# Tridiagonalisation: the next column as K times a packed vector less R, with work reordered around it

## The chip, the cores and the metric

The kernel runs on one core of one Trainium2 chip. The metric is device microseconds of one execution, as the median of several runs. A core has a matrix engine (TensorE, PE in the rows), a vector engine (VectorE, DVE), an activation engine (ScalarE, ACT), GpSimd (POOL) and a queue for transfers (SyncE, SP). They run their own instruction streams and meet at semaphores.

## The reference

Two graph layers on x of 128 batches x 128 nodes x 128 features, each behind a layer norm and a clipping at zero, and each added to x. What matters here is the first:

```
deg    = sum(A, 0) + sum(A, 1) - diag(A)
L_norm = d_inv_sqrt * (diag(deg) - A) * d_inv_sqrt
_, U   = eigh(L_norm)                     # 128 x 128, symmetric
out    = U @ (relu((U.T @ h) @ W1 + b1) @ W2 + b2)
```

The second layer is two graph convolutions and four small LSTMs over windows of 1 to 4 nodes. All is fp32.

## The kernel before

The eigenvectors are computed on the chip: the matrix is brought to tridiagonal form by 127 Householder steps (`STEPS`), the eigenvalues are found by counting sign changes and the eigenvectors by twisted factorisations, two refinements follow, and then come the two layers, batch group by batch group, with TensorE busy almost throughout. Only the tridiagonalisation is changed.

`householder(k)` exists twice, in TensorE's stream (from line 591) and in VectorE's (from line 897); ScalarE's part stands in a loop at lines 420 to 431. A step k works on the "live" columns k+1 to 127, so its row operations get shorter by one column per step. The order is written out by hand, with a semaphore for every dependence, also between two instructions of VectorE (`step()` counts them in `hv`, and `dve.wait_ge(hv, n)` waits for the n-th).

One step goes round like this:

- x, the current column below the diagonal, lies in column 128 of `ident`. VectorE writes it at L951.
- TensorE multiplies it out (L596: x's leading element and its sum of squares on all partitions; L598: the whole of x as a row).
- ScalarE takes the root of the sum (L424, `two_sigma`) and half the leading element's size (L425, `half_x`), copies the row to `uB` (L428) and stores the off-diagonal element (L431).
- VectorE forms u (L915) in `UC[:, k, 2]`; beside it lie x masked below the diagonal (`UC[:, k, 1]`, written by `prepare_sign`, L968) and minus the mask (`UC[:, k, 0]`).
- TensorE forms the row product u'A (L601, into bank 1) and A u (L603, into bank 2).
- VectorE in the meantime forms the denominator (L919, L922), the leading element of u on all partitions (`u_t`, L925), the reciprocal h (L927), and h times the three columns of UC (L930, into HB, HUM, HU).
- L935 multiplies u'A by the row of u and sums it, to K (K3). It is followed by a read of the accumulator, which has a row of its own in the trace.
- L939 to L951 work out the next column x before the matrix itself is updated: V1, Z, T2, NHP, then x. L954, L956 and L960 update the matrix A (twice) with wB between. L967, L968 (`prepare_sign`) and L974 (`prepare_row`, SGE) prepare the sign for the next u.

From step 16 on (`BN_LAG`) each step also takes the layer norm statistics of one batch, `x_statistics` (L895), which have nothing to do with the step and are put in the queue to use it. L912 forms ACOL, the next column of A below the diagonal, for T2.

Behind step 16 (`LEAF`) the leading 16 x 16 block is handed to GpSimd, which runs 16 sweeps on it beside everything else (ending with the copy at L410). VectorE reads its result, a sign, at L1343 in the second refinement.

Of the kernel before, what the change touches and what calls it, by code (L numbers as in the profile page):

```python
# [10 lines left out]
N = 128  # L11
# [19 lines left out]
SKIPS = 4  # L31
# [28 lines left out]
def build(nc, t_in, out):  # L60
    with ExitStack() as ctx:
# [3 lines left out]
        def sem(name):  # L65
            return ctx.enter_context(nc.semaphore(name))
# [58 lines left out]
        x_in = [sem(f"x_in{c}") for c in range(X_CHUNKS)]  # L125
        tables = sem("tables")
        weights_in = sem("weights_in")
        small_in = sem("small_in")
        w_turned = sem("w_turned")
        w_kept = sem("w_kept")  # L130
        small_turned = sem("small_turned")
# [39 lines left out]
        u_ready = sem("u_ready")  # L171
        p_ready = sem("p_ready")
        a_ready = sem("a_ready")
        leaf_ready = sem("leaf_ready")
        leaf_sign = sem("leaf_sign")
        to_pe = sem("to_pe")
# [11 lines left out]
        block = ctx.enter_context(nc.Block())  # L188

        STEPS = N - 1  # L190
        ST, DEN, SGE1, SGE, K3, NHP, V1, T2, Z, ACOL = range(10, 20)
        HB, HUM, HU = range(20, 23)

        def two_sigma(k):
            return sc[:, 24 + k % 2:25 + k % 2]
# [4 lines left out]
        def half_x(k):  # L200
            return sc[:, 28 + k % 2:29 + k % 2]

        def live(k):
            return slice(k + 1, N)

# [58 lines left out]
        @block.sync  # L266
        def _(sp):
            sp.dma_start(adj[:], t_in["adj"]).then_inc(adj_in, 16)
            for c in range(X_CHUNKS):
                r = slice(c * BATCH // X_CHUNKS, (c + 1) * BATCH // X_CHUNKS)  # L270
                sp.dma_start(X[:, r, :], x_dram[:, r, :]).then_inc(x_in[c], 16)
            for c, name in enumerate(("L1_gnn_Wih", "L1_gnn_Whh")):
                for p in range(SKIPS):
                    sp.dma_start(w_nat[:, c, p], t_in[name][p].rearrange("(g u) h -> u g h", g=4)).then_inc(weights_in, 16)
            for t, name in ((W1, "L0_gnn_W1"), (W2, "L0_gnn_W2"), (Wg0, "L1_gnn_Wg0"), (Wg1, "L1_gnn_Wg1")):
                sp.dma_start(t[:], t_in[name]).then_inc(small_in, 16)
            for t, name in ((b2B, "L0_gnn_b2"), (bg0B, "L1_gnn_bg0"), (bg1B, "L1_gnn_bg1")):
                sp.dma_start(t[:], t_in[name].rearrange("(a d) -> a d", a=1).to_broadcast([N, D])).then_inc(small_in, 16)
            sp.dma_start(b1[:], t_in["L0_gnn_b1"].rearrange("(d a) -> d a", a=1)).then_inc(small_in, 16)
            for c, name in enumerate(("L1_gnn_bih", "L1_gnn_bhh")):  # L280
                sp.dma_start(bias_nat[:, c, :], t_in[name].rearrange("p (g u) -> (p g) u", g=4)).then_inc(small_in, 16)
            for g in range(GROUPS):
                if g >= RING:
                    sp.wait_ge(x1_ready[g % STREAMS], (g - RING) // STREAMS + 1)
                sp.dma_start(batches(ring[g % RING]), x_dram[:, g * GB:(g + 1) * GB, :]).then_inc(ring_in[g % RING], 16)
            with nc.sync.Fori(0, ROUNDS) as it:
                for i in range(STREAMS):
                    b = bass.ds(it * (STREAMS * GB) + i * GB, GB)
                    sp.wait_ge(sum_ready[i], it + 1)
                    sp.dma_start(out_dram[:, b, :], X[:, b, :]).then_inc(stored, 16)  # L290
            sp.wait_ge(stored, 16 * ROUNDS * STREAMS)
# [124 lines left out]
        def _(act):  # L416
            act.wait_ge(rs_in, 1)
            nc.scalar.activation(m[5][:], m[4][:], ACT.Sqrt).then_inc(rs_out, 1)
            for k in range(STEPS):
                t = k + 1  # L420
                if k >= 2:
                    act.wait_ge(e_ready, k - 1)
                act.wait_ge(s_ready, k + 1)
                nc.scalar.activation(two_sigma(k), banks[7][:, 1:2], ACT.Sqrt, scale=4.0).then_inc(sigma_ready, 1)  # L424
                nc.scalar.activation(half_x(k), banks[7][:, 0:1], ACT.Abs, scale=0.5).then_inc(sigma_ready, 1)  # L425
                if t + 1 < N:
                    act.wait_ge(xb_ready, k + 1)
                    nc.scalar.activation(uB[:, k % 2, t + 1:N], banks[0][:, t + 1:N], ACT.Copy).then_inc(row_ready, 1)  # L428
                act.wait_ge(sg_ready, k + 1)
                act.wait_ge(sigma_ready, 2 * k + 1)  # L430
                nc.scalar.activation(eB[:, k:k + 1], sign(k), ACT.Identity, scale=two_sigma(k)).then_inc(e_ready, 1)  # L431
# [146 lines left out]
        def _(pe):  # L578
# [54 lines left out]
            nc.tensor.matmul(B[4], QU, QV, start=True, stop=False)  # L633
            nc.tensor.matmul(B[4], ident[:, 0:N], ident[:, 0:N], start=False, stop=True).then_inc(q_pe, 1)

            pe.wait_ge(weights_in, 16 * 2 * SKIPS)
            for c in range(2 * SKIPS):
                if c >= 2:
                    pe.wait_ge(w_kept, c - 1)
# [1 line left out]
                    last = nc.tensor.transpose(banks[c % 2][:, q * D:(q + 1) * D], w_nat[:, c // SKIPS, c % SKIPS, q, :],  # L641
                                               ident[:, 0:N])
                last.then_inc(w_turned, 1)
            pe.wait_ge(small_in, 16 * 10)
            pe.wait_ge(w_kept, 2 * SKIPS)
            nc.tensor.transpose(banks[0][:, 0:N], adj[:], ident[:, 0:N])
            K = 4 * SKIPS
# [176 lines left out]
        def _(dve):  # L824
# [4 lines left out]
            def op(ins):  # L829
                t.did(ins)  # L830
                t.last(dve)
# [8 lines left out]
            def S(i, n=1):  # L840
                return sc[:, i:i + n]
# [38 lines left out]
            V.tensor_copy(sc[:, 40:41], sc[:, 1:2]).then_inc(x_ready, 1)  # L880

            op(V.tensor_scalar(UC[:, 0:N - 1, 0], below[:, 1:N], -1.0, None, ALU.mult))
            h = Tally(hv)

            def step(ins):

                h.did(ins)
                return h.n

            def x_statistics(b):

                if b % (BATCH // X_CHUNKS) == 0:
                    dve.wait_ge(x_in[b // (BATCH // X_CHUNKS)], 16)
                V.bn_stats(stats[:, b, :], X[:, b, :]).then_inc(bn_done, 1)  # L895

            def householder(k, before):
# [8 lines left out]
                sigma2, sg = two_sigma(k), sign(k)  # L906
                x_t, s = banks[7][:, 0:1], banks[7][:, 1:2]

                if k >= BN_LAG:
                    x_statistics(k - BN_LAG)  # L910
                dve.wait_ge(a_ready, k + 1)
                step(V.tensor_tensor(S(ACOL), A[:, nxt], below[:, nxt], ALU.mult))  # L912
                dve.wait_ge(sigma_ready, 2 * k + 1)
                dve.wait_ge(hv, before)
                V.scalar_tensor_tensor(out=u_c, in0=S(SGE), scalar=sigma2, in1=x_c,  # L915
# [3 lines left out]
                n_st = step(V.tensor_scalar(S(ST), s, TINY, None, ALU.add))  # L919
                V.tensor_scalar(sg, x_t, 0.0, 0.5, ALU.is_ge, ALU.subtract).then_inc(sg_ready, 1)  # L920
                dve.wait_ge(hv, n_st)
                n_neg = step(V.scalar_tensor_tensor(out=S(DEN), in0=half_x(k), scalar=sigma2, in1=S(ST),  # L922
                                                    op0=ALU.mult, op1=ALU.add))
                dve.wait_ge(sg_ready, k + 1)
                n_ut = step(V.scalar_tensor_tensor(out=u_t, in0=sg, scalar=sigma2, in1=x_t, op0=ALU.mult, op1=ALU.add))  # L925
                dve.wait_ge(hv, n_neg)
                n_h = step(V.reciprocal(h_k, S(DEN)))  # L927
                dve.wait_ge(hv, n_h)
                dve.wait_ge(u_ready, k + 1)
                n_nh = step(V.tensor_tensor(S(HB, 3), UC[:, k, :], h_k.to_broadcast([N, 3]), ALU.mult))  # L930

                dve.wait_ge(pb_ready, k + 1)
                if t + 1 < N:
                    dve.wait_ge(row_ready, k + 1)
                n_k = step(V.tensor_tensor_reduce(out=wB[:, live(k)], in0=banks[1][:, live(k)], in1=uk[:, live(k)],  # L935
                                                  scale=h_k, scalar=0.0, op0=ALU.mult, op1=ALU.add,
                                                  accum_out=S(K3)))
                dve.wait_ge(hv, n_nh)
                n_v = step(V.tensor_tensor(S(V1), S(HB), u_t, ALU.mult))  # L939
                dve.wait_ge(hv, n_k)  # L940
                n_z = step(V.scalar_tensor_tensor(out=S(Z), in0=u_t, scalar=S(K3), in1=B[1][:, nxt],
                                                  op0=ALU.mult, op1=ALU.subtract))
                dve.wait_ge(p_ready, k + 1)
                dve.wait_ge(hv, n_v)
                n_t2 = step(V.scalar_tensor_tensor(out=S(T2), in0=banks[2][:, 0:1], scalar=S(V1), in1=S(ACOL),  # L945
                                                   op0=ALU.mult, op1=ALU.add))
                n_nhp = step(V.scalar_tensor_tensor(out=S(NHP), in0=banks[2][:, 0:1], scalar=-1.0, in1=h_k,
                                            op0=ALU.mult, op1=ALU.mult))
                dve.wait_ge(hv, n_t2)

                V.scalar_tensor_tensor(out=x_c, in0=S(HUM), scalar=S(Z), in1=S(T2),  # L951
                                       op0=ALU.mult, op1=ALU.add).then_inc(x_ready, 1)
                dve.wait_ge(hv, n_nhp)
                step(V.scalar_tensor_tensor(out=A[:, live(k)], in0=uk[:, live(k)], scalar=S(NHP), in1=A[:, live(k)],  # L954
                                                  op0=ALU.mult, op1=ALU.add))
                n_wb = step(V.scalar_tensor_tensor(out=wB[:, live(k)], in0=uk[:, live(k)], scalar=S(K3),  # L956
                                                   in1=banks[1][:, live(k)], op0=ALU.mult, op1=ALU.subtract))
                n_sge1 = prepare_sign(k + 1) if k + 1 < STEPS else None
                dve.wait_ge(hv, n_wb)
                V.scalar_tensor_tensor(out=A[:, live(k)], in0=wB[:, live(k)], scalar=S(HU), in1=A[:, live(k)],  # L960
                                       op0=ALU.mult, op1=ALU.add).then_inc(a_ready, 1)
                return prepare_row(k + 1, n_sge1) if k + 1 < STEPS else None
# [546 lines left out]
```

## Time and profile before

| what | value |
|---|---|
| median of 3 runs | 1530.33 us (1529.59 to 1530.63) |
| the profiled execution: its own time, its span | 1528.6 us, 1526.9 us |
| PE, DVE, ACT, POOL busy, share of the span | 78%, 74%, 52%, 33% |
| stretch 200 to 392 us (tridiagonalisation): PE, DVE, ACT busy | 138.74, 185.87, 46.90 us of 192 |
| stretch 674 to 1526 us (the layers): PE, DVE busy | 838.10, 479.69 us of 852 |
| TensorE's granted clock in the tridiagonalisation | 1.00 of full speed |

Times in rows are microseconds from the start of the span. An instruction's listed length is from its start to its end; instructions of one engine overlap, so that the next one can start before the listed end of the one in front. Busy time counts an engine as busy while an instruction is under way in it, also when that instruction is one element long and mostly latency.

### The profile page before, as it was taken

What the parts mean: (1) busy time and instruction counts of PE and PEld (TensorE: products, weight loads), DVE (VectorE), ACT (ScalarE), POOL (GpSimd) and SP (SyncE); (2) the same over time, 40 slices, a digit from 0 to 9 for tenths busy, and PEclk for the clock granted to TensorE, in tenths of its full rate; (3) what the DMA queues carried; (4) which work ended last, traced back from release to release, by engine and by line L of the source; (5) the groups of instructions that cost most, each with busy time, mean ns of one, the idle gap of its engine ahead of it and who ended that gap; (6) DMA issues with size and microseconds to landing.
All of it is one profiled execution on the core that took longest, in us unless ns stands there. A gap on an engine that the chain in (4) does not pass through costs nothing.

```text
span 1526.9 us, 26214 instructions
## 1 busy us (share of the span) xinstructions
PE 1196.6 (78%) x7121; PEld 1070.4 (70%) x7121; DVE 1127.4 (74%) x6077; ACT 796.6 (52%) x2572; POOL 511.0 (33%) x1426
## 2 busy tenths in 40 slices
PE   5666777777616600069999999999999999999998
PEld 4555666666515500058889899898998989989897
DVE  8999999999999999977757655555465555645545
ACT  1222222222319900002478687786877868778676
POOL 0288888888888888830000200000000000000000
PEclk9999999999959955569999999999999999999999
DMA  9300000000000000003100000000000000000001
GB/s 268 77 1 0 1 1 1 1 1 1 1 0 2 1 0 1 0 14 97 56 1 1 28 0 14 14 0 28 0 14 14 0 27 0 14 13 0 28 1 29
DMA packets 43625, 28.76 MB, mean 19 GB/s; under 512 B 1520, under 2 KB 39440, under 8 KB 43536
## 3 DMA queue, kind: packets, MB, share of 16 engines
q1 hardware_dynamic: 43536, 27.81, 6.7%
q8 instruction: 27, 0.44, 0.1%
q14 instruction: 62, 0.51, 0.1%
HBM read 19.42 MB, written 8.39 MB: 18 GB/s over the span
## 4 chain that ended last, share of the span: by engine, by line
PE 57%; DVE 38%; issue 3%; ACT 2%; ACTq 0%; DVEq 0%
PE bank L794 13%; PE bank L784 10%; PE bank L789 8%; PE bank L797 7%; PE bank L601 6%; DVE PV L1192 5%; DVE RC L1186 4%; DVE PV L1122 2%; DVE wB L935 2%; PE bank L714 2%; PE bank L766 2%; PE bank L758 2%; PE bank L722 2%; DVE sc L945 2%; PE bank L729 2%
## 5 line engine op out<-in xcount | busy, mean ns | idle before, releaser
L794 PE MATMUL bank<-spare,wT 128*128 128x256 f32 (+2 forms) x1408 | 311.2, 321 | 0.0
L530 ACT ACTIVATE PV<-bank,bias 128x256 f32<-128x256 f32 (+2 forms) x704 | 304.9, 436 | 0.0
L530 ACT ACTIVATE BIG<-bank,bias 128x128 f32<-128x128 f32 (+2 forms) x544 | 228.2, 419 | 120.2 <-PE bank L797 101.2
L794 PEld LDWEIGHTS bank<-spare,wT 128*128 128x128 f32 x1408 | 234.8, 191 | 13.2
L784 PE MATMUL bank<-spare,wT 128*128 128x128 f32 (+2 forms) x1088 | 228.1, 320 | 4.1 <-DVE spare L1429 2.7
L1415 DVE TENSOR_TENSOR BIG<-BIG,PV 128x128 f32<-128x128 f32 (+2 forms) x192 | 63.0, 328 | 206.0 <-ACT BIG L530 205.9
L784 PEld LDWEIGHTS bank<-spare,wT 128*128 128x128 f32 x1088 | 168.7, 190 | 22.5 <-DVE spare L1429 9.1
L797 PE MATMUL bank<-spare,wT 128*128 128x128 f32 (+2 forms) x768 | 169.7, 303 | 0.0
L424 ACT ACTIVATE sc<-bank 128x1 f32<-128x1 f32 x127 | 21.7, 171 | 262.3 <-PE bank L596 262.3
L596 PE MATMUL bank<-ident 128*128 128x2 f32 x254 | 74.4, 363 | 92.8 <-DVE ident L951 91.6
L789 PE MATMUL bank<-spare,wT 128*128 128x128 f32 (+2 forms) x768 | 141.6, 307 | 3.7 <-DVE spare L1427 1.2
L381 POOL TENSOR_TENSOR leaf<-leaf 128x1 f32<-128x1 f32 x240 | 136.0, 567 | 20.0
L538 ACT ACTIVATE spare<-spare 128x256 f32<-128x256 f32 (+2 forms) x352 | 134.6, 382 | 6.9 <-DVE spare L1418 6.9
L596 PEld LDWEIGHTS bank<-ident 128*128 128x128 f32 x254 | 63.7, 311 | 103.8 <-DVE ident L951 102.3
L1412 DVE TENSOR_TENSOR spare<-BIG,PV 128x256 f32<-128x256 f32 (+2 forms) x160 | 60.8, 380 | 96.2 <-ACT PV L530 96.1
L797 PEld LDWEIGHTS bank<-spare,wT 128*128 128x128 f32 x768 | 125.2, 191 | 3.3
L789 PEld LDWEIGHTS bank<-spare,wT 128*128 128x128 f32 x768 | 113.8, 191 | 14.1 <-DVE spare L1427 10.8
L379 POOL TENSOR_SCALAR leaf<-leaf 128x1 f32<-128x1 f32 x240 | 102.1, 426 | 23.3
L601 PE MATMUL bank<-A,UC 128*128 128x127 f32 (+63 forms) x254 | 87.5, 442 | 15.2 <-DVE UC L915 3.6
L588 PE MATMUL bank<-ones,sc 128*128 128x1 f32 x2 | 0.6, 349 | 120.2 <-DVE sc L1252 120.2
L601 PEld LDWEIGHTS bank<-A,UC 128*128 128x128 f32 x254 | 63.6, 311 | 38.8 <-DVE UC L915 38.8
L1192 DVE SCALAR_TENSOR_TENSOR PV<-RC,m,PV 128x4 f32<-128x4 f32 x508 | 90.7, 220 | 0.0
(393 smaller groups left out, 2756.7 us busy)
## 6 DMA issues: line engine op xcount, KB each, us to landing
spare<-in_x SPq DMA_DIRECT2D x32, 256.0 KB, 4.1
out<-X SPq DMA_DIRECT2D x32, 256.0 KB, 2.4
spare<-in_L_gnn_Wih SPq DMA_DIRECT2D x4, 256.0 KB, 5.1
spare<-in_L_gnn_Whh SPq DMA_DIRECT2D x4, 256.0 KB, 5.0
W<-in_L_gnn_W SPq DMA_DIRECT2D x2, 64.0 KB, 2.5
Wg<-in_L_gnn_Wg SPq DMA_DIRECT2D x2, 64.0 KB, 2.2
adj<-in_adj SPq DMA_DIRECT2D x1, 64.0 KB, 1.8
X<-in_x SPq DMA_DIRECT2D x4, 0.5 KB, 17.1
```

The lines of the kernel that those rows point to most:

```text
L379: op(TS(am[:, i + 1:i + 2], rho[:, i:i + 1], ne16[:, i:i + 1], am[:, i + 1:i + 2], ALU.mult, ALU.add))
L381: op(TT(rho[:, i + 1:i + 2], am[:, i + 1:i + 2], neg16[:, 0:1], ALU.pow))
L530: last = nc.scalar.activation(gate_out[q][i][:, 0:T], gate(i, q, T), ACT.Tanh if q == GATE_G else ACT.Sigmoid, bias=bias[:, at:at + 1])
L538: nc.scalar.activation(tS[i][:, 0:T], cS[i][:, 0:T], ACT.Tanh).then_inc(tanh_ready[i], 1)
L596: nc.tensor.matmul(banks[7][:, 0:2], x_wide, ident[:, t:N + 1:N - t], start=True, stop=True).then_inc(s_ready, 1)
L601: nc.tensor.matmul(banks[1][:, live(k)], u_c.to_broadcast([N, N]), A[:, live(k)], start=True, stop=True).then_inc(pb_ready, 1)
L784: last = nc.tensor.matmul(gate(i, q, T), wT[:, 0, p - 1, q * D:(q + 1) * D], xt, start=True, stop=(j == 0))
L789: last = nc.tensor.matmul(gate(i, q, T), wT[:, 1, p - 1, q * D:(q + 1) * D], hS[i][:, 0:T], start=False, stop=True)
L794: last = nc.tensor.matmul(gate(i, q, T), wT[:, 0, p - 1, q * D:(q + 1) * D], xt, start=True, stop=(j == 0))
L797: last = nc.tensor.matmul(gate(i, q, T), wT[:, 1, p - 1, q * D:(q + 1) * D], hS[i][:, 0:T], start=False, stop=True)
L1192: s.did(V.scalar_tensor_tensor(out=nx, in0=RC[:, last + lane:last + lane + live], scalar=M[2][:, row:row + 1], in1=nx, op0=ALU.mult, op1=A ...
L1415: V.tensor_tensor(gI[i][:, 0:T], gI[i][:, 0:T], gG[i][:, 0:T], ALU.mult).then_inc(cell_part[i], 1)
```

## The change

- L912 (ACOL) leaves VectorE. ScalarE computes it as a copy of A's column with the mask column as its scale, between L425 and the copy of the row; it waits for `a_ready`. A semaphore `acol_ready` tells VectorE.
- `UC[:, k, 0]` holds the mask instead of minus the mask.
- The product of h with three columns becomes two instructions: HUM, HU = h times two columns, and HV, HG = u_t times h times (mask, masked x), a tensor_scalar with two scalars that are read from columns.
- The next column was HUM * (u_t K - b) + (p V1 + ACOL), b being the element of bank 1, in four instructions behind K (V1, Z, T2, x). It becomes HG * K - R, with PT = b * HUM - ACOL, R = p * HV + PT: three instructions behind K.
- NHP is computed behind x instead of in front of it; wB comes before A's first update instead of behind it.
- `x_statistics` moves from the start of the step to behind the reciprocal; the wait for ScalarE's copy of the row (`row_ready`) moves from L935 to the product in front of it.
- ScalarE's wait for its own stores (`e_ready`) goes, and the loads of the small weights count on the semaphore of the large ones; TensorE waits for all of them at once, behind the eigenvectors' preparation.

```diff
 # ScalarE
-                if k >= 2:
-                    act.wait_ge(e_ready, k - 1)
                 act.wait_ge(s_ready, k + 1)
                 nc.scalar.activation(two_sigma(k), banks[7][:, 1:2], ACT.Sqrt, scale=4.0).then_inc(sigma_ready, 1)
                 nc.scalar.activation(half_x(k), banks[7][:, 0:1], ACT.Abs, scale=0.5).then_inc(sigma_ready, 1)
+                act.wait_ge(a_ready, k + 1)
+                nc.scalar.activation(S_(ACOL), A[:, t:t + 1], ACT.Copy, scale=below[:, t:t + 1]).then_inc(acol_ready, 1)
 # TensorE
-            pe.wait_ge(weights_in, 16 * 2 * SKIPS)
+            pe.wait_ge(weights_in, 16 * (2 * SKIPS + 10))
...
-            pe.wait_ge(small_in, 16 * 10)
 # VectorE
-            op(V.tensor_scalar(UC[:, 0:N - 1, 0], below[:, 1:N], -1.0, None, ALU.mult))
+            op(V.tensor_copy(UC[:, 0:N - 1, 0], below[:, 1:N]))
...
-                if k >= BN_LAG:
-                    x_statistics(k - BN_LAG)
-                dve.wait_ge(a_ready, k + 1)
-                step(V.tensor_tensor(S(ACOL), A[:, nxt], below[:, nxt], ALU.mult))
                 dve.wait_ge(sigma_ready, 2 * k + 1)
...
                 n_h = step(V.reciprocal(h_k, S(DEN)))
+                if k >= BN_LAG:
+                    x_statistics(k - BN_LAG)
                 dve.wait_ge(hv, n_h)
                 dve.wait_ge(u_ready, k + 1)
-                n_nh = step(V.tensor_tensor(S(HB, 3), UC[:, k, :], h_k.to_broadcast([N, 3]), ALU.mult))
-
-                dve.wait_ge(pb_ready, k + 1)
                 if t + 1 < N:
                     dve.wait_ge(row_ready, k + 1)
-                n_k = step(V.tensor_tensor_reduce(out=wB[:, live(k)], in0=banks[1][:, live(k)], in1=uk[:, live(k)],
-                                                  scale=h_k, scalar=0.0, op0=ALU.mult, op1=ALU.add,
-                                                  accum_out=S(K3)))
-                dve.wait_ge(hv, n_nh)
-                n_v = step(V.tensor_tensor(S(V1), S(HB), u_t, ALU.mult))
-                dve.wait_ge(hv, n_k)
-                n_z = step(V.scalar_tensor_tensor(out=S(Z), in0=u_t, scalar=S(K3), in1=B[1][:, nxt],
-                                                  op0=ALU.mult, op1=ALU.subtract))
+                n_hu = step(V.tensor_tensor(S(HUM, 2), UC[:, k, 1:3], h_k.to_broadcast([N, 2]), ALU.mult))
+                n_hv = step(V.tensor_scalar(S(HV, 2), UC[:, k, 0:2], u_t, h_k, ALU.mult, ALU.mult))
+
+                dve.wait_ge(pb_ready, k + 1)
+                dve.wait_ge(acol_ready, k + 1)
+                step(V.tensor_tensor_reduce(out=wB[:, live(k)], in0=banks[1][:, live(k)], in1=uk[:, live(k)],
+                                            scale=h_k, scalar=0.0, op0=ALU.mult, op1=ALU.add, accum_out=S(K3)))
+                dve.wait_ge(hv, n_hu)
+                n_pt = step(V.scalar_tensor_tensor(out=S(PT), in0=B[1][:, nxt], scalar=S(HUM), in1=S(ACOL),
+                                                   op0=ALU.mult, op1=ALU.subtract))
+                dve.wait_ge(hv, n_pt)
                 dve.wait_ge(p_ready, k + 1)
-                dve.wait_ge(hv, n_v)
-                n_t2 = step(V.scalar_tensor_tensor(out=S(T2), in0=banks[2][:, 0:1], scalar=S(V1), in1=S(ACOL),
-                                                   op0=ALU.mult, op1=ALU.add))
+                n_r = step(V.scalar_tensor_tensor(out=S(R), in0=banks[2][:, 0:1], scalar=S(HV), in1=S(PT),
+                                                  op0=ALU.mult, op1=ALU.add))
+                dve.wait_ge(hv, n_r)
+                V.scalar_tensor_tensor(out=x_c, in0=S(HG), scalar=S(K3), in1=S(R),
+                                       op0=ALU.mult, op1=ALU.subtract).then_inc(x_ready, 1)
                 n_nhp = step(V.scalar_tensor_tensor(out=S(NHP), in0=banks[2][:, 0:1], scalar=-1.0, in1=h_k,
-                                            op0=ALU.mult, op1=ALU.mult))
-                dve.wait_ge(hv, n_t2)
-
-                V.scalar_tensor_tensor(out=x_c, in0=S(HUM), scalar=S(Z), in1=S(T2),
-                                       op0=ALU.mult, op1=ALU.add).then_inc(x_ready, 1)
-                dve.wait_ge(hv, n_nhp)
-                step(V.scalar_tensor_tensor(out=A[:, live(k)], in0=uk[:, live(k)], scalar=S(NHP), in1=A[:, live(k)],
-                                                  op0=ALU.mult, op1=ALU.add))
+                                                    op0=ALU.mult, op1=ALU.mult))
                 n_wb = step(V.scalar_tensor_tensor(out=wB[:, live(k)], in0=uk[:, live(k)], scalar=S(K3),
                                                    in1=banks[1][:, live(k)], op0=ALU.mult, op1=ALU.subtract))
+                dve.wait_ge(hv, n_nhp)
+                n_a = step(V.scalar_tensor_tensor(out=A[:, live(k)], in0=uk[:, live(k)], scalar=S(NHP), in1=A[:, live(k)],
+                                                  op0=ALU.mult, op1=ALU.add))
```

## Rows read from the trace of the kernel before

**Rows 1.** The chain of work that ended last, stretch 13 to 392 us, shares by line

```profile
by line: PE bank L601 22.7%; DVE wB L935 8.7%; DVE sc L945 7.3%; issue 6.8%; DVE ident L951 6.4%; DVE A L960 6.0%; DVE UC L915 6.0%; DVE A L954 6.0%; DVE wB L956 5.8%; DVE sc L912 3.7%; PE bank L596 2.7%; DVE sc L939 2.3%; DVE sc L947 2.2%;
```

**Rows 2.** Line L951: count, ns shortest/median/longest, first and last start

```profile
L951 DVE SCALAR_TENSOR_TENSOR ident<-sc x127: 211/219/278, 14.6 to 391.2; 128x1 f32<-128x1 f32 x127
```

**Rows 3.** Order of time, one step near 65 columns: start, length, engine, line, operation

```profile
206.41 0.22 DVE L951 SCALAR_TENSOR_TENSOR ident<-sc 128x1 f32<-128x1 f32 x1
206.55 0.28 DVE L954 SCALAR_TENSOR_TENSOR A<-uB,sc,A 128x66 f32<-128x66 f32 x1
...
207.07 0.28 DVE L960 SCALAR_TENSOR_TENSOR A<-wB,sc,A 128x66 f32<-128x66 f32 x1
...
207.27 0.15 DVE L974 TENSOR_TENSOR sc<-sc,ident 128x1 f32<-128x1 f32 x1
207.34 0.28 DVE L895 BATCH_NORM_STATS2 stats<-X 128x6 f32<-128x128 f32 x1
207.36 0.17 ACT L424 ACTIVATE sc<-bank 128x1 f32<-128x1 f32 x1 [2.00 <-PE bank L596]
...
207.54 0.14 DVE L912 TENSOR_TENSOR sc<-A,below 128x1 f32<-128x1 f32 x1
207.60 0.21 DVE L915 SCALAR_TENSOR_TENSOR UC<-sc,ident 128x1 f32<-128x1 f32 x1
...
207.86 0.69 PE L601 MATMUL bank<-A,UC 128*128 128x65 f32 x2
...
208.17 0.16 DVE L927 RECIPROCAL hB<-sc 128x1 f32<-128x1 f32 x1
...
208.37 0.16 DVE L930 TENSOR_TENSOR sc<-UC,hB 128x3 f32<-128x3 f32 x1
208.59 0.28 DVE L935 CUSTOM_DVE_ANT_0 wB<-bank,uB,hB 128x65 f32<-128x65 f32 x1
208.80 0.08 DVE L935 DVE_READ_ACCUMULATOR2_ANT sc<- 128x1 f32 x1
...
209.06 0.22 DVE L945 SCALAR_TENSOR_TENSOR sc<-bank,sc 128x1 f32<-128x1 f32 x1
209.19 0.15 DVE L947 SCALAR_TENSOR_TENSOR sc<-bank,hB 128x1 f32<-128x1 f32 x1
209.31 0.22 DVE L951 SCALAR_TENSOR_TENSOR ident<-sc 128x1 f32<-128x1 f32 x1
```

**Rows 4.** Order of time, VectorE, a step near 106 columns

```profile
80.21 0.22 DVE L951 SCALAR_TENSOR_TENSOR ident<-sc 128x1 f32<-128x1 f32 x1
...
81.53 0.21 DVE L915 SCALAR_TENSOR_TENSOR UC<-sc,ident 128x1 f32<-128x1 f32 x1
...
82.59 0.33 DVE L935 CUSTOM_DVE_ANT_0 wB<-bank,uB,hB 128x106 f32<-128x106 f32 x1
```

**Rows 5.** Order of time, VectorE, a step at 14 columns

```profile
351.83 0.22 DVE L951 SCALAR_TENSOR_TENSOR ident<-sc 128x1 f32<-128x1 f32 x1
...
353.00 0.22 DVE L915 SCALAR_TENSOR_TENSOR UC<-sc,ident 128x1 f32<-128x1 f32 x1
...
353.91 0.23 DVE L935 CUSTOM_DVE_ANT_0 wB<-bank,uB,hB 128x14 f32<-128x14 f32 x1
```

**Rows 6.** Order of time, VectorE, step 15, which has no statistics

```profile
59.07 0.22 DVE L951 SCALAR_TENSOR_TENSOR ident<-sc 128x1 f32<-128x1 f32 x1
...
60.33 0.22 DVE L915 SCALAR_TENSOR_TENSOR UC<-sc,ident 128x1 f32<-128x1 f32 x1
...
61.41 0.33 DVE L935 CUSTOM_DVE_ANT_0 wB<-bank,uB,hB 128x112 f32<-128x112 f32 x1
```

**Rows 7.** Order of time, VectorE, a tensor_scalar with two scalars from columns

```profile
662.34 0.29 DVE L1335 TENSOR_SCALAR sc<-sc 128x2 f32<-128x2 f32 x1
```

**Rows 8.** Order of time, the end of GpSimd's leaf work and VectorE's first reading

```profile
662.45 0.21 POOL L410 COPY leaf<-leaf 128x1 f32<-128x1 f32 x1 [0.23 <-POOL leaf L408]
...
670.56 0.21 DVE L1343 SCALAR_TENSOR_TENSOR sc<-sc,leaf 128x1 f32<-128x1 f32 x1
```

More of the change, by code:

```diff
@@ L127, in build @@
         weights_in = sem("weights_in")
-        small_in = sem("small_in")
         w_turned = sem("w_turned")
@@ L173, in build @@
         a_ready = sem("a_ready")
+        acol_ready = sem("acol_ready")
         leaf_ready = sem("leaf_ready")
@@ L190, in build @@
         STEPS = N - 1
-        ST, DEN, SGE1, SGE, K3, NHP, V1, T2, Z, ACOL = range(10, 20)
-        HB, HUM, HU = range(20, 23)
+        ST, DEN, SGE1, SGE, K3, NHP, PT, R, ACOL = range(10, 19)
+        HUM, HU, HV, HG = range(20, 24)
         def two_sigma(k):
@@ L204, in live, with S_ @@
             return slice(k + 1, N)
+        def S_(i):
+            return sc[:, i:i + 1]
         d16, e16 = leaf[:, 0:16], leaf[:, 16:32]
@@ L275, in _ @@
             for t, name in ((W1, "L0_gnn_W1"), (W2, "L0_gnn_W2"), (Wg0, "L1_gnn_Wg0"), (Wg1, "L1_gnn_Wg1")):
-                sp.dma_start(t[:], t_in[name]).then_inc(small_in, 16)
+                sp.dma_start(t[:], t_in[name]).then_inc(weights_in, 16)
             for t, name in ((b2B, "L0_gnn_b2"), (bg0B, "L1_gnn_bg0"), (bg1B, "L1_gnn_bg1")):
-                sp.dma_start(t[:], t_in[name].rearrange("(a d) -> a d", a=1).to_broadcast([N, D])).then_inc(small_in, 16)
-            sp.dma_start(b1[:], t_in["L0_gnn_b1"].rearrange("(d a) -> d a", a=1)).then_inc(small_in, 16)
+                sp.dma_start(t[:], t_in[name].rearrange("(a d) -> a d", a=1).to_broadcast([N, D])).then_inc(weights_in, 16)
+            sp.dma_start(b1[:], t_in["L0_gnn_b1"].rearrange("(d a) -> d a", a=1)).then_inc(weights_in, 16)
             for c, name in enumerate(("L1_gnn_bih", "L1_gnn_bhh")):
-                sp.dma_start(bias_nat[:, c, :], t_in[name].rearrange("p (g u) -> (p g) u", g=4)).then_inc(small_in, 16)
+                sp.dma_start(bias_nat[:, c, :], t_in[name].rearrange("p (g u) -> (p g) u", g=4)).then_inc(weights_in, 16)
             for g in range(GROUPS):
@@ L921, in householder @@
                 dve.wait_ge(hv, n_st)
-                n_neg = step(V.scalar_tensor_tensor(out=S(DEN), in0=half_x(k), scalar=sigma2, in1=S(ST),
+                n_den = step(V.scalar_tensor_tensor(out=S(DEN), in0=half_x(k), scalar=sigma2, in1=S(ST),
                                                     op0=ALU.mult, op1=ALU.add))
@@ L925, in householder @@
                 n_ut = step(V.scalar_tensor_tensor(out=u_t, in0=sg, scalar=sigma2, in1=x_t, op0=ALU.mult, op1=ALU.add))
-                dve.wait_ge(hv, n_neg)
+                dve.wait_ge(hv, n_den)
                 n_h = step(V.reciprocal(h_k, S(DEN)))
+                if k >= BN_LAG:
+                    x_statistics(k - BN_LAG)
                 dve.wait_ge(hv, n_h)
                 dve.wait_ge(u_ready, k + 1)
-                n_nh = step(V.tensor_tensor(S(HB, 3), UC[:, k, :], h_k.to_broadcast([N, 3]), ALU.mult))
@@ L956, in householder @@
                 n_wb = step(V.scalar_tensor_tensor(out=wB[:, live(k)], in0=uk[:, live(k)], scalar=S(K3),
                                                    in1=banks[1][:, live(k)], op0=ALU.mult, op1=ALU.subtract))
+                dve.wait_ge(hv, n_nhp)
+                n_a = step(V.scalar_tensor_tensor(out=A[:, live(k)], in0=uk[:, live(k)], scalar=S(NHP), in1=A[:, live(k)],
+                                                  op0=ALU.mult, op1=ALU.add))
                 n_sge1 = prepare_sign(k + 1) if k + 1 < STEPS else None
-                dve.wait_ge(hv, n_wb)
+                dve.wait_ge(hv, max(n_a, n_wb))
```

## Prediction, made before the change was run

> **What bounds the kernel now.** I read the chain that ended last first, limited to the tridiagonalisation: it alternates between TensorE's product for p (L601) and a long tail of small VectorE instructions [rows 1]. There is one such loop for each of 127 steps, and L951, which writes the new column x, runs from 14.6 to 391.2 us, so a step is (391.2 - 14.6) / 126 = 2.99 us [rows 2]. What follows this stage is VectorE work again, so each microsecond of the stage goes to the end. Next I read single steps in order of time, and cut one at three instructions: x (L951), u (L915), the row product with its sum K (L935).
>
> The step with some 65 live columns [rows 3] has these stretches. **x to u** takes 1.19 us (206.41 to 207.60). Two ways run side by side: the matmul and ACT's root L424, which starts 0.95 after x, lasts 0.17 and hands over in 0.04 (the gap between L601's end at 208.55 and L935 at 208.59), so 1.16; and VectorE's own queue, which gets to u at 1.19. With 106 columns the stretch takes 1.32, with 14 it takes 1.17 [rows 4, 5]: above some 65 columns VectorE's queue sets it, below that the floor of 1.16. **u to K** takes 0.99 and ends 0.04 behind L601, so TensorE sets it; 1.06 with many columns, 0.91 with few [rows 3 to 5], because L601 gets shorter. VectorE has slack there: it starts L930 at 208.37 and could go on. **K to x** takes 0.72.
>
> Three habits of VectorE are to be seen in [rows 3]. An independent instruction starts 0.08 us before the listed end of the one in front: L912 is 0.14 long and L915 starts 0.06 later; statistics are 0.28 long and L912 starts 0.20 later. One that reads the result of the one in front starts 0.04 behind its end (L927, 0.16 long, to L930: 0.20). An instruction with one scalar read from a column is 0.21 to 0.22 long at one element (L915, L945), and one with a constant 0.15 (L947).
>
> **Part 1, x to u.** Behind x the queue is now NHP, wB, A's first update, the sign work, A's second update, SGE, u. NHP starts 0.14 after x, as L954 does now; wB 0.07 later (0.15 - 0.08). wB and the first update only change places, so from the first of them to L960 it stays 0.52 (206.55 to 207.07). L960 to L974 is 0.20, and u, which reads L974's result, comes 0.15 + 0.04 = 0.19 later. Sum 0.14 + 0.07 + 0.52 + 0.20 + 0.19 = 1.12. That is under the floor, so the floor of 1.16 holds: gain 0.03 at 65 columns. The stretch grew by 0.13 from there to 106 columns (1.32 - 1.19), so the new sum there is 1.12 + 0.13 = 1.25: gain 0.07. At 14 columns the floor already holds: gain 0. The first 16 steps have no statistics: 1.26 now [rows 6], by the same sum with 112 columns 1.27: I call it nothing. The statistics (0.20) and L912 (0.06) leave this stretch, but NHP (0.07) comes in and the wait for SGE (0.12 more than its spacing of 0.07), which statistics had covered, is laid bare.
>
> **Part 2, u to K.** L915 to the reciprocal L927 is 0.57 and unchanged. Behind it now: the statistics (0.16 - 0.08 = 0.08 after L927), the product for HUM and HU (0.20 later), HV and HG (0.08 later, by L930's 0.16), and K's instruction. HV and HG come from one instruction with two scalars read from columns, u_t and h. The step has none, but the trace does, later: L1335 on two elements is 0.29 long [rows 7], so its follower comes 0.21 later. Sum 0.57 + 0.08 + 0.20 + 0.08 + 0.21 = 1.14, and VectorE, not TensorE, sets the stretch. The gap behind the reciprocal that statistics are to fill is only 0.20 wide, and they take 0.28 of queue there; the slack in front of K was 0.22 at most (208.37 to 208.59), and HV eats it. Loss: 1.14 - 1.06 = 0.08 at 106 columns, 0.15 at 65, 0.23 at 14. Without statistics (first 16 steps) it is 0.57 + 0.20 + 0.08 + 0.21 = 1.06 against 1.08 now [rows 6]: hidden behind L601.
>
> HV's price is the term that decides. From below it is 0.07, the spacing of an instruction with constants; from above the 0.21. I take 0.21, since L1335 is the same form on the same number of elements, and one scalar from a column visibly costs 0.06 to 0.07 here, spacing included. 
>
> **Part 3, K to x.** Three dependent instructions: PT starts with the read of the accumulator, 0.21 after K's instruction; R 0.21 + 0.04 = 0.25 later; x another 0.25 later. Sum 0.71 against 0.72. The present order has five instructions there, but the last pair, T2 to x, is already 0.25 apart (209.06 to 209.31) with NHP inside the gap, so taking NHP and V1 away shortens nothing. R reads p no earlier than T2 did. I take 0.01 per step, 1.3 us.
>
> **Part 4, the rest.** ACT's new multiplication for ACOL needs A's second update, which ends at 207.35, just as L424 starts, and is first read behind K at 208.80: over a microsecond of cover. Queued behind it on ACT is the copy of x's row, which HUM's instruction now waits for; if that came late, each 0.1 us would cost 11 us over 111 steps, but both operands are there early. The wait for e_ready on ACT names old stores and ended nothing. The single weight semaphore delays TensorE only behind this stage, when those loads are long over.
>
> **Sum.** Net per step: 0.08 - 0.07 = +0.01 at 106 columns (step 21), 0.15 - 0.03 = +0.12 at 65 (step 62), +0.23 at 14 (step 113), about +0.25 at the last. With straight lines between: 5 x 0.01 + 41 x 0.065 + 51 x 0.175 + 13 x 0.24 = 14.8 us, less 1.3: **+13.5 us**. The profiled execution took 1528.6 us, so 1542.1; the median of the runs is 1.7 above that execution: **1544 us**. A loss here is exposed whole. A gain after step 16 would not be: GpSimd's leaf work, started behind step 16, ends at 662.66, and VectorE reads its sign at 670.56 [rows 8], so 7.9 us of gain at most.
>
> **Rivals.**
> - *HV as cheap as with constants* (0.07). Then u to K is 1.00: losses 0, 0.01 and 0.09, net -0.07, -0.02, +0.09. Sum -0.3 - 1.8 + 1.8 + 1.3 - 1.3 = about 0: 1530 us, no change. This is what the page's 75 ns would make of it. Against it: L1335's length. Chance 0.14.
> - *Faster: the statistics vanish in the gap behind the reciprocal, and HV is cheap.* u to K by VectorE is 0.57 + 0.20 + 0.07 + 0.07 = 0.91, never above TensorE's, and only part 1's gain is left: -3.2 - 1.3 = -4.5, under the cap of 7.9: 1526 us. It decides once that stretch takes under about 1.00. For it: the gap is as wide as the statistics' spacing. Against it: the reciprocal's own 0.08 comes first. Chance 0.12.
> - *Slower still: HUM's instruction starts only when the statistics are complete* (0.28 + 0.04 instead of 0.20), or part of that, because it has three waits. Up to 0.12 x 111 = 13 us more, 1557; half of it 1551. Against it: nothing it reads comes from them. Chance 0.12.
> - The forecast: 0.62.
>
> Slower by over 0.2% (3 us, about what a measurement can tell from no change) gets 0.62 + 0.12 = 0.74, within 0.2% 0.14, faster 0.12. The likeliest case alone spans 1536 to 1548. The range of 8 in 10 reaches down to the no-change case and up past half of the last rival: 1528 to 1553.
>
> **What the changed profile would show.** x to u: 1.25 and then flat at 1.16 to 1.17 from about 75 columns down; that would hold part 1. u to K: flat at about 1.14 whatever the columns, with L601 long done; if it still shrinks with the columns, HV is cheap and the forecast wrong. HV's instruction 0.29 long with K's 0.21 behind it. K to x unchanged. ACOL's activation done before u. The stage from 14.6 to about 405 instead of 391 us.

## The result and the profile after

The changed kernel takes 1537.88 us (median of 5 runs, 1537.44 to 1538.21) against 1530.15: ratio 1.005, interval 1.0039 to 1.0062, so 7.7 us slower. The profiled execution took 1537.93 us with a span of 1536.2. One of the ten executions of after_stats_front below took 2912.92 us; why is open, and it is left out of that kernel's ratio.

First the line that writes x, as in [rows 2], then the chain by line in the same stage, as in [rows 1], both of the kernel after:

```profile
L947 DVE SCALAR_TENSOR_TENSOR ident<-sc x127: 219/220/269, 14.6 to 399.0; 128x1 f32<-128x1 f32 x127
```

```profile
by line: PE bank L599 9.8%; DVE sc L944 7.5%; DVE ident L947 7.5%; DVE UC L913 7.2%; DVE sc L933 6.8%; issue 6.7%; DVE sc L920 6.2%; DVE wB L937 5.3%; DVE sc L940 4.7%; DVE stats L897 4.4%; DVE sc L932 4.3%; DVE A L958 3.8%; DVE A L954 3.8%
```

The last x is written 7.8 us later (399.0 against 391.2), as much as the loss of the medians. The two profiled executions themselves are 9.3 apart (1537.93 against 1528.6); the other 1.5 lies behind this stage, where the rest of the program takes 1135.7 to 1137.4 us in all the traces but that of three_edits, without order, and is not put down to the change. TensorE's row product, 22.7% of the stage's chain before, is gone from the head of it, and the new HV (L933), the statistics (L897) and HUM (L932) are in the chain. So from step 16 on the chain between u and K no longer goes through TensorE. A step near 65 columns, VectorE in order of time (to be laid beside [rows 3]; L947 x, L949 NHP, L951 wB, L958 A's second update, L972 SGE, L913 u, L925 reciprocal, L937 K, L940 PT, L944 R):

```profile
211.72 0.25 DVE L947 SCALAR_TENSOR_TENSOR ident<-sc 128x1 f32<-128x1 f32 x1
211.89 0.14 DVE L949 SCALAR_TENSOR_TENSOR sc<-bank,hB 128x1 f32<-128x1 f32 x1
211.96 0.27 DVE L951 SCALAR_TENSOR_TENSOR wB<-uB,sc,bank 128x65 f32<-128x65 f32 x1
...
212.47 0.28 DVE L958 SCALAR_TENSOR_TENSOR A<-wB,sc,A 128x65 f32<-128x65 f32 x1
212.67 0.15 DVE L972 TENSOR_TENSOR sc<-sc,ident 128x1 f32<-128x1 f32 x1
212.92 0.22 DVE L913 SCALAR_TENSOR_TENSOR UC<-sc,ident 128x1 f32<-128x1 f32 x1
...
213.51 0.16 DVE L925 RECIPROCAL hB<-sc 128x1 f32<-128x1 f32 x1
213.58 0.28 DVE L897 BATCH_NORM_STATS2 stats<-X 128x6 f32<-128x128 f32 x1
213.77 0.14 DVE L932 TENSOR_TENSOR sc<-UC,hB 128x2 f32<-128x2 f32 x1
213.83 0.30 DVE L933 TENSOR_SCALAR sc<-UC,uB,hB 128x2 f32<-128x2 f32 x1
214.03 0.28 DVE L937 CUSTOM_DVE_ANT_0 wB<-bank,uB,hB 128x64 f32<-128x64 f32 x1
...
214.23 0.21 DVE L940 SCALAR_TENSOR_TENSOR sc<-bank,sc 128x1 f32<-128x1 f32 x1
214.48 0.22 DVE L944 SCALAR_TENSOR_TENSOR sc<-bank,sc 128x1 f32<-128x1 f32 x1
214.73 0.22 DVE L947 SCALAR_TENSOR_TENSOR ident<-sc 128x1 f32<-128x1 f32 x1
```

HV is 0.30 long and K's instruction comes 0.20 behind it (the medians over all steps with statistics are 0.28 and 0.19). u to K is 1.11 (212.92 to 214.03), K to x 0.70, x to u 1.20. And u starts 0.25 behind SGE (212.67 to 212.92), not 0.19. A late step, at 14 columns (to be laid beside [rows 5]; L425 is ScalarE's root, L604 the row product):

```profile
358.74 0.25 DVE L947 SCALAR_TENSOR_TENSOR ident<-sc 128x1 f32<-128x1 f32 x1
...
359.04 0.59 PE L599 MATMUL bank<-ident 128*128 128x2 f32 x2 [0.83 <-DVE ident L947]
359.67 0.17 ACT L425 ACTIVATE sc<-bank 128x1 f32<-128x1 f32 x1 [2.06 <-PE bank L599]
359.87 0.22 DVE L913 SCALAR_TENSOR_TENSOR UC<-sc,ident 128x1 f32<-128x1 f32 x1 [0.19 <-ACT sc L425]
360.14 0.60 PE L604 MATMUL bank<-A,UC 128*128 128x14 f32 x2
...
360.97 0.22 DVE L937 CUSTOM_DVE_ANT_0 wB<-bank,uB,hB 128x14 f32<-128x14 f32 x1
```

Here too u to K takes 1.10, though the row product had ended at 360.74, 0.23 earlier. The root starts 0.04 behind the matmul's end (359.63 to 359.67). That leads to a number nobody had asked for: the floor of x to u is now 1.10 and was 1.16 (medians; the step shown has 1.13).

Cutting all steps at x, u and K gives the medians of the three stretches, in us (from the start of every instruction in the order-of-time view; the last four columns are kernels of the experiments below):

| steps | before | after | statistics front | waits swapped | two edits | three edits |
|---|---|---|---|---|---|---|
| x to u, 1 to 15 | 1.29 | 1.34 | 1.35 | 1.28 | 1.28 | 1.21 |
| x to u, 17 to 29 | 1.32 | 1.31 | 1.33 | 1.24 | 1.25 | 1.18 |
| x to u, 30 to 44 | 1.30 | 1.27 | 1.30 | 1.19 | 1.20 | 1.17 |
| x to u, 60 to 74 | 1.20 | 1.17 | 1.19 | 1.17 | 1.11 | 1.11 |
| x to u, 90 to 104 | 1.16 | 1.10 | 1.11 | 1.17 | 1.10 | 1.10 |
| u to K, 17 to 29 | 1.06 | 1.10 | 1.06 | 1.12 | 1.07 | 1.07 |
| u to K, 60 to 74 | 0.99 | 1.10 | 1.03 | 1.10 | 1.00 | 0.99 |
| u to K, 105 to 126 | 0.91 | 1.10 | 1.05 | 1.11 | 0.92 | 0.92 |
| K to x, 60 to 74 | 0.72 | 0.70 | 0.70 | 0.70 | 0.72 | 0.72 |

Summed over steps 1 to 126, after less before: x to u -3.2, u to K +14.2, K to x -3.2, together +7.8 us.

### The profile page after: what moved, and what is told of

Read it like the earlier page. It is cut to its first block, busy times and chain, and to the rows that moved or that the text cites. A ratio compares the mean times of both kernels' runs of the same rounds, so it can differ in the third digit from the quotient of the medians.

```text
span 1536.2 us, 26089 instructions
## 1 busy us (share of the span) xinstructions
PE 1197.6 (78%) x7121; PEld 1071.5 (70%) x7121; DVE 1124.8 (73%) x5950; ACT 822.4 (54%) x2699; POOL 500.4 (33%) x1426
## 4 chain that ended last, share of the span: by engine, by line
PE 53%; DVE 41%; ACT 3%; issue 3%; DVEq 0%; ACTq 0%
PE bank L796 13%; PE bank L786 9%; PE bank L791 8%; PE bank L799 7%; DVE PV L1190 5%; DVE RC L1184 4%; PE bank L599 3%; DVE PV L1120 2%; PE bank L716 2%; PE bank L768 2%; DVE sc L944 2%; DVE ident L947 2%; PE bank L724 2%; PE bank L760 2%; DVE UC L913 2%
## 5 line engine op out<-in xcount | busy, mean ns | idle before, releaser
L425 ACT ACTIVATE sc<-bank 128x1 f32<-128x1 f32 x127 | 21.7, 171 | 264.7 <-PE bank L599 264.7
L604 PE MATMUL bank<-A,UC 128*128 128x127 f32 (+63 forms) x254 | 87.5, 442 | 12.7 <-DVE UC L913 2.3
L382 POOL TENSOR_SCALAR leaf<-leaf 128x1 f32<-128x1 f32 x240 | 88.1, 367 | 23.4
L604 PEld LDWEIGHTS bank<-A,UC 128*128 128x128 f32 x254 | 63.6, 311 | 36.3 <-DVE UC L913 36.3
```

What stands on the lines that cost most here:

```text
L382: op(TS(am[:, i + 1:i + 2], rho[:, i:i + 1], ne16[:, i:i + 1], am[:, i + 1:i + 2], ALU.mult, ALU.add))
L604: nc.tensor.matmul(banks[1][:, live(k)], u_c.to_broadcast([N, N]), A[:, live(k)], start=True, stop=True).then_inc(pb_ready, 1)
```

## The experiments

Each was measured beside the kernel before, whose median was 1529.8 to 1529.9 in these.

**before_no_e and before_e_second.** What lowered the floor? The change took one wait of ScalarE away that names old stores.

```diff
-                if k >= 2:
-                    act.wait_ge(e_ready, k - 1)
                 act.wait_ge(s_ready, k + 1)
```

> The kernel before without ScalarE's wait for e_ready in front of the root. Theory A (a wait in front of the one that ends last delays the instruction by some 0.06 us): the floor of x to u falls from 1.16 to 1.10, which counts where the floor binds, from about step 75 on: 52 x 0.06 = 3 us less, 1527 us. Theory B (the wait names old stores and costs nothing, as predicted): 1530.

Measured: 1527.20 us against 1529.87, ratio 0.9986 (0.9976 to 0.9995). x to u is 1.10 in steps 105 to 126, 1.34 and unchanged within 0.02 in steps 17 to 29. Theory A holds, and my sentence that this wait ended nothing falls. In the second kernel the wait stays but stands behind the other:

> The kernel before with ScalarE's two waits in the other order, s_ready first and e_ready second. If only the order counts (the wait that ends last must stand first): as without e_ready, 1527 us. If the number of waits counts: 1530.

Measured: 1527.29 us, ratio 0.9981 (0.9972 to 0.9991), floor 1.10 again. So it isn't the number of waits. A late step of it, x, matmul, root, u:

```profile
350.00 0.59 PE L596 MATMUL bank<-ident 128*128 128x2 f32 x2 [0.58 <-DVE ident L951]
350.62 0.17 ACT L424 ACTIVATE sc<-bank 128x1 f32<-128x1 f32 x1 [1.81 <-PE bank L596]
350.83 0.22 DVE L915 SCALAR_TENSOR_TENSOR UC<-sc,ident 128x1 f32<-128x1 f32 x1
```

The root starts 0.03 behind the matmul's end (350.59 to 350.62). In the kernel before it was 0.10, here in the step of [rows 5]:

```profile
352.10 0.59 PE L596 MATMUL bank<-ident 128*128 128x2 f32 x2 [0.58 <-DVE ident L951]
352.79 0.17 ACT L424 ACTIVATE sc<-bank 128x1 f32<-128x1 f32 x1 [1.87 <-PE bank L596]
```

What counts is that the wait that ends last is the first of the two in the program.

**after_with_e.** The same from the other side: the wait put back into the changed kernel.

> The changed kernel with ScalarE's wait for e_ready put back in front of s_ready. Theory A: the floor of x to u rises from 1.10 to 1.16, from about step 75 on: 2.9 us more than the changed kernel, 1540.8. Theory B (no effect there): 1537.9.

Measured: 1540.64 us, ratio to before 1.0069 (1.0052 to 1.0086), so 2.8 above the changed kernel; the floor is 1.16 again. The change thus holds a gain of some 3 us that is not of its arithmetic.

**after_waits_swapped.** Is it the same on VectorE? u waits for ScalarE's root and for SGE, in this order.

```diff
-                dve.wait_ge(sigma_ready, 2 * k + 1)
                 dve.wait_ge(hv, before)
+                dve.wait_ge(sigma_ready, 2 * k + 1)
```

> The changed kernel with u's two waits on VectorE in the other order, SGE's first and ScalarE's root second. Theory A (the wait that ends last must stand first): x to u 0.06 shorter where SGE comes last, some 60 steps, and 0.06 longer where the root does, some 45 steps: about 1 us less than the changed kernel, with the stretches moved in opposite directions. Theory B (order is nothing on VectorE): every stretch unchanged.

Measured: 1536.09 us, ratio 1.0044 (1.0027 to 1.0061). The time hardly moves, but the table shows that the stretches move in opposite directions, as theory A has it: x to u 1.31 to 1.24 in steps 17 to 29 and 1.10 to 1.17 in steps 90 to 104. An early and a late step of this kernel (L425 the root, L972 SGE, L913 u):

```profile
80.95 0.15 DVE L972 TENSOR_TENSOR sc<-sc,ident 128x1 f32<-128x1 f32 x1
81.14 0.22 DVE L913 SCALAR_TENSOR_TENSOR UC<-sc,ident 128x1 f32<-128x1 f32 x1
...
358.07 0.17 ACT L425 ACTIVATE sc<-bank 128x1 f32<-128x1 f32 x1 [1.97 <-PE bank L599]
358.34 0.22 DVE L913 SCALAR_TENSOR_TENSOR UC<-sc,ident 128x1 f32<-128x1 f32 x1 [0.21 <-ACT sc L426]
```

u starts 0.04 behind SGE's end (81.10 to 81.14), which was 0.10 in the changed kernel, and now 0.10 behind the root's end (358.24 to 358.34), which was 0.03.

**after_hv_twice.** HV's price, by doubling it.

```diff
                 n_hv = step(V.tensor_scalar(S(HV, 2), UC[:, k, 0:2], u_t, h_k, ALU.mult, ALU.mult))
+                step(V.tensor_scalar(S(30, 2), UC[:, k, 0:2], u_t, h_k, ALU.mult, ALU.mult))
```

> The changed kernel with a second instruction like HV's, to two columns that nobody reads. Theory A (two scalars from columns cost 0.19 to 0.20): u to K 1.30 in all steps with statistics, 1.24 without: 111 x 0.19 + 16 x 0.14 = 23 us more, 1561. Theory B (75 ns per instruction): 9 us more, 1547.

Measured: 1560.17 us, 22.3 above the changed kernel (ratio to before 1.0200, 1.0183 to 1.0217). One step, VectorE, the two and K's instruction (L938):

```profile
227.73 0.28 DVE L897 BATCH_NORM_STATS2 stats<-X 128x6 f32<-128x128 f32 x1
227.92 0.14 DVE L932 TENSOR_TENSOR sc<-UC,hB 128x2 f32<-128x2 f32 x1
227.98 0.28 DVE L933 TENSOR_SCALAR sc<-UC,uB,hB 128x2 f32<-128x2 f32 x1
228.17 0.28 DVE L934 TENSOR_SCALAR sc<-UC,uB,hB 128x2 f32<-128x2 f32 x1
228.36 0.28 DVE L938 CUSTOM_DVE_ANT_0 wB<-bank,uB,hB 128x63 f32<-128x63 f32 x1
```

0.19 from one to the next, where the product with a broadcast operand in front of them (L932) takes 0.06. The Trainium skill (Vector Engine (DVE) Microarchitecture Reference, section 5.2, "Measured stream behaviour on trn2") gives about 75 ns per instruction, taken from long instructions, and says nothing there of scalars that are read from columns. An estimate from that figure is 9.5 us for the 127 instructions. The trace is near it for L932's kind (0.06) and far from it for an instruction with two scalars from columns (0.19, and 22.3 us in all).

**before_stats_back and after_stats_front.** The statistics alone, in either kernel. In the first they move behind the reciprocal and nothing else changes:

```diff
-                if k >= BN_LAG:
-                    x_statistics(k - BN_LAG)
                 dve.wait_ge(a_ready, k + 1)
...
                 n_h = step(V.reciprocal(h_k, S(DEN)))
+                if k >= BN_LAG:
+                    x_statistics(k - BN_LAG)
```

> The kernel before, with the statistics alone moved behind the reciprocal. Theory A (HV with its two scalars is what costs, not the statistics): u to K on VectorE is 0.59 + 0.07 + 0.19 + 0.07 = 0.92, under TensorE's 0.91 to 1.06 nearly everywhere, and x to u loses 0.03 to 0.10 in steps 16 to 75: 1526 us. Theory B (the statistics lengthen u to K whatever stands behind them): 111 x 0.07 = 8 us more less 4, 1534.

Measured: 1526.59 us, ratio 0.9979 (0.9969 to 0.9989). Steps 17 to 29: x to u 1.25, u to K 1.07, so the gain is in the first and the second is covered. In a step near 65 columns of this kernel (L913 u, L925 reciprocal, L930 the product with three columns, L935 K):

```profile
207.83 0.22 DVE L913 SCALAR_TENSOR_TENSOR UC<-sc,ident 128x1 f32<-128x1 f32 x1
...
208.10 0.69 PE L601 MATMUL bank<-A,UC 128*128 128x64 f32 x2
...
208.41 0.16 DVE L925 RECIPROCAL hB<-sc 128x1 f32<-128x1 f32 x1
208.48 0.28 DVE L895 BATCH_NORM_STATS2 stats<-X 128x6 f32<-128x128 f32 x1
208.68 0.15 DVE L930 TENSOR_TENSOR sc<-UC,hB 128x3 f32<-128x3 f32 x1
208.83 0.28 DVE L935 CUSTOM_DVE_ANT_0 wB<-bank,uB,hB 128x64 f32<-128x64 f32 x1
```

L930 comes 0.27 behind the reciprocal instead of 0.20, and K's instruction is still 1.00 behind u: it starts 0.04 behind the end of the row product (208.79 to 208.83), so TensorE still sets it. The second puts the statistics of the changed kernel back in front of u's waits:

> The changed kernel with the statistics back in front of u. Theory A (there they fill the wait for SGE, 0.25 wide, and cost 0.01 to 0.02; behind the reciprocal they cost 0.07 in front of an already late HV): u to K 1.03 to 1.06 instead of 1.10, 7 us less, x to u 1 us more: 1532 us. Theory B (their 0.19 comes whole onto x to u where VectorE sets it, some 60 steps): 11 us more less 7: 1541.

Measured: 1533.05 us, ratio 1.0020 (1.0010 to 1.0030), 4.8 below the changed kernel. u to K falls to 1.03 to 1.06, x to u rises by 0.01 to 0.03 up to step 74. So the same move gains 3.3 us in one kernel and loses 4.8 in the other: behind the reciprocal there is room for the statistics or for HV, not for both.

**best.** The column as in the change, statistics in front of u, u's waits by which ends last, and HV without scalars from columns.

```diff
+                dve.wait_ge(hv, n_ut)
+                n_g = step(V.tensor_tensor(S(GV, 2), UC[:, k, 0:2], u_t.to_broadcast([N, 2]), ALU.mult))
...
-                n_hv = step(V.tensor_scalar(S(HV, 2), UC[:, k, 0:2], u_t, h_k, ALU.mult, ALU.mult))
+                dve.wait_ge(hv, n_g)
+                step(V.tensor_tensor(S(HV, 2), S(GV, 2), h_k.to_broadcast([N, 2]), ALU.mult))
```

> The changed kernel with the statistics in front of u, u's waits ordered by which ends last (SGE first in the first 16 steps), and HV, HG as two broadcast products: u_t times the two columns under the reciprocal, then times h. Theory A: u to K is 0.59 + 0.31 + 0.06 = 0.97 on VectorE, so TensorE sets it until about step 80; x to u as before in early steps and 0.06 less in late ones; K to x 0.02 to 0.03 less: 1525. Theory B (the extra instruction and wait cost as much as the two scalars did): u to K 1.03, as with the statistics in front, 1533.

Measured: 1529.22 us, ratio 0.9997 (0.9987 to 1.0007): no change, neither theory's number. Behind the reciprocal (L931) stand the u_t product, HUM, HV and K (L944):

```profile
210.06 0.15 DVE L931 RECIPROCAL hB<-sc 128x1 f32<-128x1 f32 x1
210.17 0.18 DVE L933 TENSOR_TENSOR sc<-UC,uB 128x2 f32<-128x2 f32 x1
210.28 0.17 DVE L938 TENSOR_TENSOR sc<-UC,hB 128x2 f32<-128x2 f32 x1
210.39 0.16 DVE L940 TENSOR_TENSOR sc<-sc,hB 128x2 f32<-128x2 f32 x1
210.51 0.28 DVE L944 CUSTOM_DVE_ANT_0 wB<-bank,uB,hB 128x64 f32<-128x64 f32 x1
```

Each has a wait of its own here, and they come 0.11 to 0.12 apart in this step (0.09 to 0.12 in the medians), not 0.06; that the waits are the reason was not tried. u to K is 1.00 to 1.02 in the medians instead of 0.97. The sum over steps, less before: x to u -2.8, u to K +4.7, K to x -1.9, together 0. With HV as one instruction and the statistics in front (after_stats_front) u to K was +7.2, so two products with broadcast operands in HV's place give back 2.5 us.

**two_edits and three_edits.** The old column arithmetic with what had proved a gain. The third edit is ACOL on ScalarE as in the change (with VectorE's wait for it in front of the product with h, and the small weights on the large ones' semaphore), and with it goes a new order of u's waits: SGE's first up to step 44, the root's first from step 45 on. Their shares were not separated.

> The kernel before with two edits: statistics behind the reciprocal, and ScalarE's wait for e_ready gone. Theory A (the two gains lie in different steps, the first where VectorE sets x to u, the second where the root does, and add up): 1523 us. Theory B (the cap: GpSimd's leaf work ends too late for more than one of them): 1526.

Measured: 1522.31 us, ratio 0.9952 (0.9938 to 0.9965), near theory A. But the gains do not lie in different steps only: alone they are 2.7 and 3.3 us, together 7.5. In steps 60 to 74 x to u is 1.20 before, 1.19 without the wait for e_ready, 1.16 with the statistics behind, and 1.11 with both, since each edit alone shortens one of two ways that are nearly equally long there. VectorE reads the leaf's sign at 663.25, 1.2 us behind the end of the leaf work.

> The same two edits, and ACOL on ScalarE, with u's wait for SGE in front of the root's up to step 44 and behind it from there on. VectorE's column arithmetic stays as before, with no instruction of two scalars. x to u 1.19 in steps 17 to 30, 1.14 in 30 to 45 and 1.10 behind, u to K set by TensorE: 1519 us by theory A (the gains reach the end). Theory B (VectorE now waits for the leaf sign): 1522 or more, with idle time in front of the reading of the sign.

Measured: 1521.24 us, ratio 0.9942 (0.9929 to 0.9956). The last x is written at 380.6 us, 3.1 before that of two_edits (383.7), yet the median moves by 1.1 only, and the two profiled executions took the same (1521.59 and 1521.32). GpSimd's leaf work and VectorE's reading of its sign, in three_edits (to be laid beside [rows 8]):

```profile
662.74 0.18 POOL L410 COPY leaf<-leaf 128x1 f32<-128x1 f32 x1 [0.23 <-POOL leaf L408]
662.96 0.22 DVE L1344 SCALAR_TENSOR_TENSOR sc<-sc,leaf 128x1 f32<-128x1 f32 x1 [2.63 <-POOL leaf L410]
```

VectorE stood idle for 2.63 us: theory B in mechanism, at a number between the two. Both versions beat the kernel before and the changed one.

## Why the prediction was right, and where its sizes were off

The direction and its cause hold. Forecast were +13.5 us and 1544; measured +7.7 and 1537.88, inside 1528 to 1553, but at little over half of the size. Step by step:

- **u to K** was to become flat at 1.14 with VectorE setting it, 18.0 us more in sum (14.8 + 3.2). It is flat at 1.10 from step 16 on and gives 14.2. HV's price was right (0.21 taken, 0.19 to 0.20 measured, L1335 being the fit row). Mis-sized were the small spacings: I took 0.08 for the reciprocal and for HUM's instruction where [rows 3] already showed 0.06 behind L912, and the trace has 0.07, 0.19, 0.06, 0.19 where I summed 0.08, 0.20, 0.08, 0.21. Against these 0.06, u to the reciprocal is 0.59 and not 0.57. That leaves 0.04 in 111 steps, 4 us. Of the loss 4.8 us belong to the place of the statistics, as after_stats_front shows.
- **x to u** was to give 3.2 and gives 3.2, by luck: two errors cancel. The wait for SGE costs 0.25 and not 0.19, since SGE's is the second of u's waits: no gain in steps 17 to 29 but 0.01, and 0.05 lost in the first 15, where I had written nothing; with the waits swapped these are back at 1.28. Against it, the floor sank from 1.16 to 1.10. By steps, 1 to 15, 16 to 62 and 63 to 126, the sums forecast are 0, 2.4 and 0.8 us gained, and those of the trace -1.2, 1.2 and 3.1. The sentence that e_ready "ended nothing" is the step that was wrong in kind; it is worth 3 us.
- **K to x** was to lose 0.01 per step and loses 0.02, and the sum 3.2 instead of 1.3. About 1 us of it is not of the arithmetic in every step: in steps 40, 50, 104, 109 and 114 K to x takes 0.80 to 0.96 in the kernel before, and in the same steps of before_no_e, before_e_second, before_stats_back and two_edits, and the changed kernel has one such step, 98, with 0.90. What holds these steps up is open. That T2 to x was already a dependent pair, so that fewer instructions shorten next to nothing, holds: PT, R and x are 0.25 apart (214.23, 214.48, 214.73).
- **ScalarE.** One sign did not come: ACOL's activation ends 0.16 behind the start of u (median), not before it. It costs nothing, since it is done 0.9 before K's instruction in every step, and the copy of the row is done at least 0.13 before HUM's.
- **The cap** of gains by GpSimd was not touched by a slower kernel, but three_edits ran into it.

Of the rivals, the cheap HV falls by the doubling, and with it the faster one. The slower one (HUM's instruction waiting for the whole of the statistics) falls by 0.19 between them.

## What to carry to other kernels

In a chain of one-element instructions, count start-to-start distances by form, not instructions: one fewer saved 0.02 here, since those left are each 0.25 behind their producer, and one that reads two scalars from columns took 0.19 where one with a broadcast operand and no wait behind it took 0.06. A move into a gap must be priced together with everything else that the change puts into that gap. Where an instruction has two waits, put the one that ends last first. Where two ways are about equally long, shorten both before judging either.

## What the runs showed of the hardware that was not expected

- **Order of two waits.** An instruction with two waits started 0.03 to 0.04 us after the event of its first wait and 0.09 to 0.10 after that of its second, if that ended last. This was so on ScalarE (0.10 against 0.04 in the medians) and on VectorE in both directions. Why it is so was not tried.
- **GpSimd's leaf work has no fixed length.** It starts at 65.55 us in the kernel before and ends at 662.66; in the changed kernel it runs from 66.84 to 653.29, and in best from 65.23 to 663.88, with the same GpSimd program each time. So it took 597, 586 and 599 us. It is not the VectorE program alone: before_no_e and before_e_second have that of the kernel before, and the leaf work took 593 and 595 us in them; with the changed kernel's VectorE program it took 586 and, in after_with_e, 590. What sets it is open.
